# A two-layer transformer kernel on one core: who evicts the second attention's keys, queries and values

## The chip, the cores and the metric

The kernel runs on 1 core of one Trainium2 chip. The metric is the time of one execution on the device in microseconds (us), lower is better. Engines are named as in the profile: PE is TensorE (PEld its weight loads), DVE VectorE, ACT ScalarE, POOL GpSimd, SP SyncE.

## What is computed

2048 tokens of width 128 pass two layers. The first mixes in the frequency domain and has a gated feed-forward block; the second is plain attention over all 2048 tokens with 16 heads of width 8, then a mixture of 8 experts. Only the beginning of the second attention matters here:

```python
h = layernorm(x) * (1 + ca) + sa                 # 2048 x 128
qkv = einsum('bnd,ed->bne', h, qkv_w) + qkv_b
q, k, v = split(qkv.reshape(b, n, 16, 3 * 8), 3) # per head
attn = softmax(einsum('bhqd,bhkd->bhqk', q, k) * 8 ** -0.5)
out = einsum('bhqk,bhkd->bhqd', attn, v)
```

## The kernel before, in words

One program per engine, written out by hand; semaphores order the engines. Numbers of lines are those of the profile.

**The products.** Keys and queries are made as 32 "stacks": a stack is one f32 product of 128x512 (L787), for one of four head groups `hg` and one block `tb` of 512 tokens. In each head's 32 rows stand three copies of its 8 numbers, which carry a two-part (high and low) form: ScalarE copies the product with a mask as scale into `hi`, rounded to fp32r (L506), and VectorE computes product + bias - `hi` into `Ks` or `Qs` (L1257). The list `stacks` gives their order. The values are 16 tiles of 128x256, two to a PSUM bank (L796, `value_tiles`); VectorE adds the bias row `vb1` on the way into `V` (L1263). Stacks and values rotate through the PSUM banks 4 to 7.

**The first maxima.** The softmax needs the maximum of each query's scores before its main loop. `nat(k, pair)` on TensorE makes two 128x512 score products of 32 rows each (L811) in one of two pairs of banks; `maxima(k, pair)` on VectorE reduces them with one instruction over 1024 columns (L1269). Key positions k run from 0; 21 of them (`LEAD`), so 42 of these pairs, come before the main loop. I call the place of one pair a slot: slot 2k + pair. After k = 15 VectorE reduces the row maxima once more (`maximum(0)`), GpSimd splits them (`split_max(0)`), TensorE transposes them (`max_rows(0)`), ScalarE copies them to `mT`, and two DMAs from SP's queue put them into rows of `Qb`.

**The order.** Five stacks come first (`early`), then ScalarE copies the first queries into `Qb` and the slots begin. The function `between(slot)` says which of the other 27 stacks and the 8 pairs of value tiles stand behind which of the first 32 slots; TensorE and VectorE both follow it. Slots 32 to 41 have no such work; there `keep_busy` puts products without use between the pairs (46 of 128x512, L851, two of them directly ahead of the loop). The loop (`step(s)`, 256 steps) takes scores, exponentials on ScalarE into `probs`, products with `V`, and goes on with the maxima of later key positions.

Of the kernel before, what the change touches and what calls it, by code (L numbers as in the profile page):

```python
# [12 lines left out]
F32 = mybir.dt.float32  # L13
F32R = mybir.dt.float32r
BF16 = mybir.dt.bfloat16
ALU = mybir.AluOpType
# [3 lines left out]
P = 128  # L20
# [15 lines left out]
VW = 16  # L36
# [27 lines left out]
x2_ready kq_ready kq_hi kq_done v_ready v_copied q_filled busy_done bank_ready bank_read rows_read m_top m_step  # L64
# [5 lines left out]
def adaln_pair(nc, x_in, consts_in, mods_in, spectral_in, ffn_in, attn_in, moe_in, out):  # L70
    with ExitStack() as ctx:
        def sb(name, shape, dt=F32, where=ctx):
            return where.enter_context(nc.sbuf_tensor(name, shape, dt))
# [79 lines left out]
        with l1:  # L153
            Ks = sb("Ks", [P, HG, TOK], F32R, where=l1)
            Qs = sb("Qs", [P, HG, TOK], F32R, where=l1)
            Qb = sb("Qb", [P, HG, 512], F32R, where=l1)
            V = sb("V", [P, NT, H1 * VW], where=l1)
            hi = sb("hi", [P, 2, 512], F32R, where=l1)
            probs = sb("probs", [P, 16, 512], where=l1)
            mx = sb("mx", [P, 2, 4, 4, G4], where=l1)  # L160
            mn = sb("mn", [P, 16], where=l1)
            m2 = sb("m2", [P, 4, 8], where=l1)
            mhi = sb("mhi", [P, 16], F32R, where=l1)
            mT = sb("mT", [8, 512], F32R, where=l1)
            U = sb("U", [P, 512], where=l1)
            rden = sb("rden", [P, 4, G4], where=l1)

        l2 = ExitStack()
        with l2:
# [15 lines left out]
            gtT = sb("gtT", [8, 512], where=l2)  # L185
            acc = sb("acc", [P, 4, P], where=l2)


        def columns(tensor, pack):
            at, views = 0, {}  # L190
# [23 lines left out]
        def due(count):  # L214

            return not isinstance(count, int) or count > 0
# [43 lines left out]
        def wait_turn(engine, *what):  # L260
# [9 lines left out]
            + [(1, hg, 0) for hg in range(1, HG)] + [(0, hg, tb) for hg in range(2, HG) for tb in range(TB)] \  # L270
            + [(1, hg, tb) for hg in range(HG) for tb in range(1, TB)]
        early = 5

        def between(slot):
# [3 lines left out]
            n = len(stacks)  # L278
            return range(min(lo, n), min(hi_, n)), range(max(lo, n) - n, max(hi_, n) - n)


        groups = [(ri, j) for ri in range(2) for j in range(KV)]
# [31 lines left out]
        def _(pool):  # L314
# [32 lines left out]
            for hg in range(1, HG):  # L347
                pool.wait_ge(sem.kq_done, stacks.index((1, hg, 0)) + 1)
                fill(0, hg)
            split_max(0)  # L350
            pool.wait_ge(sem.kq_done, len(stacks))
            for grp in range(1, 16):
                split_max(grp)
# [5 lines left out]
        def _(act):  # L359
# [139 lines left out]
            ln_out(2)  # L499

            act.wait_ge(sem.attn_in, 16)
            for n, (kq, hg, tb) in enumerate(stacks):
                act.wait_ge(sem.kq_ready, n + 1)
                if due(n - 1):
                    act.wait_ge(sem.kq_done, n - 1)
                act.activation(hi[:, n % 2, :], bank(4 + n % 4), ACT.Identity, bias=(kb_lo, qb_lo)[kq][:, hg:hg + 1],  # L506
                               scale=cw[("lo_k", "lo_q")[kq]]).then_inc(sem.kq_hi, 1)
                if n == early - 1:

                    act.wait_ge(sem.kq_done, early)  # L510
                    act.activation(Qb[:, 0, :], Qs[:, 0, 0:512].bitcast(F32), ACT.Copy).then_inc(sem.first_filled, 1)


            def copy_max_rows(grp):

# [21 lines left out]
            copy_max_rows(0)  # L537
            for s in range(256):
                exps(s)
            act.wait_ge(sem.pv_ready, 256)  # L540
# [60 lines left out]
        def _(pe):  # L601
# [180 lines left out]

            def stack(n):
                kq, hg, tb = stacks[n]
                if due(n - 3):
                    pe.wait_ge(sem.kq_done, n - 3)
                pe.matmul(bank(4 + n % 4), aw[("kw1", "qw1")[kq]][:, hg * P:hg * P + P],  # L787
                          hT[:, tb * 512:tb * 512 + 512], start=True, stop=True).then_inc(sem.kq_ready, 1)

            def value_tiles(u):  # L790
                pe.wait_ge(sem.kq_done, min(len(stacks), len(stacks) - 3 + u))
                if due(u - 3):
                    pe.wait_ge(sem.v_copied, u - 3)
                for i in range(2):
                    t = 2 * u + i
                    last = pe.matmul(ps[:, 4 + u % 4, 256 * i:256 * i + 256], hT[:, t * P:t * P + P], aw["vw1"],  # L796
                                     start=True, stop=True)
                last.then_inc(sem.v_ready, 1)

            def nat(k, pair):  # L800
# [95 lines left out]
            for n in range(early):  # L896
                stack(n)
            pe.wait_ge(sem.kq_done, early)
            for k in range(16):
                for half in range(2):  # L900
                    nat(k, half)
                    some_stacks, some_values = between(2 * k + half)
                    for n in some_stacks:
                        stack(n)
                    for u in some_values:
                        value_tiles(u)
            pe.wait_ge(sem.v_copied, NT // 2 - 2)
            keep_busy(8)
            pe.wait_ge(sem.v_copied, NT // 2)
            for k in range(16, LEAD):  # L910
                for pair in range(2):
                    nat(k, pair)
# [112 lines left out]
        def _(dve):  # L1025
# [225 lines left out]
            ln_stats(2, TB - 1)  # L1251
            ln(2)

            def stack(n):
                kq, hg, tb = stacks[n]
                dve.wait_ge(sem.kq_hi, n + 1)
                dve.scalar_tensor_tensor(out=(Ks, Qs)[kq][:, hg, tb * 512:tb * 512 + 512], in0=bank(4 + n % 4),  # L1257
                                         scalar=(kb_one, aw["qb1"])[kq][:, hg:hg + 1], in1=hi[:, n % 2, :].bitcast(F32),
                                         op0=ALU.add, op1=ALU.subtract).then_inc(sem.kq_done, 1)

            def value_tiles(u):
                dve.wait_ge(sem.v_ready, u + 1)
                dve.tensor_tensor(V[:, 2 * u:2 * u + 2, :], bank(4 + u % 4).rearrange("p (t n) -> p t n", t=2),  # L1263
                                  wide(aw["vb1"], [P, 2, H1 * VW], 1), ALU.add).then_inc(sem.v_copied, 1)

            def maxima(k, pair):
                at = turn_bank("nat", k, pair)
                dve.wait_ge(sem.bank_ready, turn_at["nat", k, pair] + 1)
# [32 lines left out]
                if kt == turn_kt and s > 16:  # L1301
                    normalise(grp)

            for n in range(early):
                stack(n)
            for k in range(16):
                for half in range(2):
                    maxima(k, half)
                    some_stacks, some_values = between(2 * k + half)
                    for n in some_stacks:  # L1310
                        stack(n)
                    for u in some_values:
                        value_tiles(u)
            maximum(0)
            for pair in range(2):
                maxima(16, pair)

            dve.wait_ge(sem.v_copied, NT // 2)
            dve.memset(bank(6), 0.0).then_inc(sem.u_zero, 1)
            for k in range(17, LEAD):  # L1320
                for pair in range(2):
                    maxima(k, pair)
            for s in range(256):
                step(s)
            normalise(16)
# [182 lines left out]
```

## Time and profile before

| | us |
|---|---|
| median of three runs | 1224.33 |
| lowest and highest | 1223.57, 1225.33 |
| the profiled execution | 1223.92 |
| its span, first to last instruction | 1222.1 |
| VectorE busy | 829.3 (68%) |
| ScalarE busy | 813.3 (67%) |
| GpSimd busy | 28.9 (2%) |
| TensorE busy | 1129.2 (92%) |
| mean granted TensorE clock | 0.974 |

Times of instructions below are microseconds from the span's start. The difference of the profiled time and its span, 1.8 us, lies outside the first and last instruction.

### The profile page before, as it was taken

To read this page: it belongs to the slowest core of one execution; us is meant where nothing else is said; L and a number is where in the kernel's file an instruction comes from. 1 tells how busy PE (TensorE), PEld (TensorE's weight loads), DVE (VectorE), ACT (ScalarE), POOL (GpSimd) and SP (SyncE) were. 2 spreads that over 40 slices of the span, in tenths; PEclk is the share of its full clock that TensorE was granted. 3 is DMA by queue.
4 is the path that set the end of the run, shared out by engine and by line. 5 is a ranking of instruction groups with operands and counts; after the bars stand their busy time and mean duration, and the time that the engine had idled before them with its cause. 6 is when DMAs were issued, how large, how long until landed. Compare 5 with 4: busy or idle time off the path is not lost.

```text
span 1222.1 us, 21866 instructions
## 1 busy us (share of the span) xinstructions
PE 1129.2 (92%) x9020; PEld 634.8 (52%) x9020; DVE 829.3 (68%) x1172; ACT 813.3 (67%) x1495; POOL 28.9 (2%) x73
## 2 busy tenths in 40 slices
PE   4865999888999999999999999999999699999998
PEld 3534788732533333333333333333333379798887
DVE  3857333369999999999999999999930622222222
ACT  2646443344089999989999999999898554444342
POOL 0002000000000000000000000000000000000000
PEclk9996999979989999999999999999999899999999
DMA  9000000000000000000000000000000000000000
GB/s 383 21 1 0 1 1 1 1 0 1 1 2 2 2 2 2 1 2 2 2 2 2 2 2 2 2 2 2 2 2 2 1 1 1 10 1 9 6 3 9
DMA packets 5432, 14.84 MB, mean 12 GB/s; under 512 B 352, under 2 KB 4576, under 8 KB 4832
## 3 DMA queue, kind: packets, MB, share of 16 engines
q1 hardware_dynamic: 5056, 10.84, 2.3%
q10 hardware_dynamic: 288, 2.76, 0.5%
q8 instruction: 64, 1.05, 0.3%
q14 instruction: 24, 0.20, 0.1%
HBM read 12.29 MB, written 1.05 MB: 11 GB/s over the span
## 4 chain that ended last, share of the span: by engine, by line
DVE 48%; PE 46%; ACT 4%; issue 1%; DMA 1%; SPq 0%; DVEq 0%; ACTq 0%
DVE mx L1269 41%; PE ps L990 9%; PE ps L721 6%; PE ps L722 6%; PE ps L723 6%; PE ps L870 4%; PE ps L842 4%; PE ps L758 1%; PE ps L811 1%; PE ps L971 1%; PE ps L787 1%; DMA x<-x_in 1%; PE ps L851 1%; DVE Qs L1257 1%; DVE z L1042 1%
## 5 line engine op out<-in xcount | busy, mean ns | idle before, releaser
L1269 DVE TENSOR_REDUCE mx<-ps 128x2 f32<-128x1024 f32 x512 | 587.7, 1213 | 14.8 <-PE ps L811 14.1
L534 ACT ACTIVATE probs<-ps 128x512 f32<-128x512 f32 x1024 | 540.7, 598 | 57.3 <-PE ps L870 48.3
L870 PE MATMUL ps<-Qb,Ks 32*128 32x512 f32 x1024 | 328.7, 496 | 0.5 <-ACT probs L534 0.5
L842 PE MATMUL ps<-probs,V 128*16 128x256 f32 x4096 | 320.6, 386 | 7.1 <-ACT U L528 7.1
L811 PE MATMUL ps<-Ks,Qb 32*128 32x512 f32 x1024 | 257.3, 499 | 8.2 <-DVE mx L1269 5.2
L870 PEld LDWEIGHTS ps<-Qb,Ks 32*128 32x128 f32 x1024 | 150.5, 182 | 214.7 <-issue 124.7
L581 ACT ACTIVATE eh<-ps,MW 128x512 f32<-128x512 f32 x128 | 87.5, 688 | 83.4 <-PE ps L723 82.9
L842 PEld LDWEIGHTS ps<-probs,V 128*16 128x16 f32 x4096 | 67.2, 94 | 134.1 <-issue 76.5
L990 PEld LDWEIGHTS ps<-MW,eh 128*128 128x128 f32 x1024 | 118.3, 192 | 2.4
L811 PEld LDWEIGHTS ps<-Ks,Qb 32*128 32x128 f32 x1024 | 95.3, 182 | 46.1 <-DVE mx L1269 32.0
L990 PE MATMUL ps<-MW,eh 128*128 128x128 f32 x1024 | 119.2, 275 | 0.0
L1388 DVE SCALAR_TENSOR_TENSOR acc<-ps,gate,acc 128x128 f32<-128x128 f32 x128 | 36.0, 344 | 121.5 <-PE ps L990 121.1
L721 PE MATMUL ps<-hT,ew 128*128 (+1 forms) x128 | 53.1, 415 | 0.0
L1224 DVE TENSOR_TENSOR act_b<-bf,act_b 128x512 fp32r<-128x512 f32 x16 | 11.1, 692 | 58.9 <-ACT bf L478 58.9
L722 PE MATMUL ps<-hT,ew 128*128 (+1 forms) x128 | 50.1, 391 | 0.0
L723 PE MATMUL ps<-hT,ew 128*128 (+1 forms) x128 | 50.0, 390 | 0.0
L787 PE MATMUL ps<-hT,AW 128*128 128x512 f32 x64 | 38.5, 703 | 0.9 <-ACT hT L375 0.9
L1286 DVE RECIPROCAL rden<-ps 128x16 f32<-128x16 f32 x16 | 4.1, 257 | 49.3 <-PE ps L828 48.9
L484 ACT ACTIVATE act_c<-ps,FW 128x512 f32<-128x512 f32 x16 | 11.0, 686 | 27.5 <-PE ps L723 27.5
L721 PEld LDWEIGHTS ps<-hT,ew 128*128 128x128 f32 x128 | 24.1, 188 | 7.7 <-issue 3.4
L574 ACT ACTIVATE rh<-ps,MW 128x512 f32<-128x512 f32 x16 | 10.9, 688 | 24.8 <-PE ps L723 24.8
L711 PE MATMUL ps<-CW,z 128*128 128x128 f32 x48 | 12.5, 432 | 15.9 <-DVE z L1042 15.9
(218 smaller groups left out, 1085.9 us busy)
## 6 DMA issues: line engine op xcount, KB each, us to landing
MW<-moe_in SPq DMA_DIRECT2D x1, 4454.0 KB, 23.9
FW<-ffn_in SPq DMA_DIRECT2D x1, 2824.5 KB, 12.5
SW<-spectral_in ACTq DMA_DIRECT2D x1, 1479.5 KB, 9.9
DW<-mods_in ACTq DMA_DIRECT2D x1, 1219.0 KB, 6.4
x<-x_in SPq DMA_DIRECT2D x4, 256.0 KB, 10.9
out<-x SPq DMA_DIRECT2D x4, 256.0 KB, 2.3
AW<-attn_in SPq DMA_DIRECT2D x1, 836.5 KB, 13.8
Qb<-mT SPq DMA_DIRECT2D x32, 8.0 KB
```

The source lines that it names most:

```text
L534: act.activation(probs[:, 4 * (s % 4) + g, :], score(n), ACT.Exp, scale=SCALE1) \
L581: act.activation(eh[:, e % 2, fb, :], up_bank(fb), ACT.Relu, bias=mw["eb1"][:, col:col + 1]).then_inc(sem.eh_copied, 1)
L721: pe.matmul(to, w[0], v[0], start=start, stop=False)
L722: pe.matmul(to, w[0], v[1], start=False, stop=False)
L723: return pe.matmul(to, w[1], v[0], start=False, stop=stop)
L787: pe.matmul(bank(4 + n % 4), aw[("kw1", "qw1")[kq]][:, hg * P:hg * P + P], hT[:, tb * 512:tb * 512 + 512], start=True, stop=True).then_inc ...
L811: last = pe.matmul(bank(turn_bank("nat", k, pair) + g % 2), Qb[rows, hg, qt * P:qt * P + P], Ks[rows, hg, c * 512:c * 512 + 512], start=Tr ...
L842: last = pe.matmul(ps[32 * g:32 * g + VW, 6, queries], V[:, kt, col:col + VW], probs[:, 4 * (s % 4) + g, queries], start=(kt == 0 and half ...
L870: pe.matmul(score(n), Ks[rows, hg, kt * P:kt * P + P], Qb[rows, hg, :], start=True, stop=True).then_inc(sem.st_ready, 1)
L990: last = pe.matmul(ps[:, 2 + e % 2, qt * P:qt * P + P], eh[:, e % 2, fb, qt * P:qt * P + P], mw["ew2"][:, col:col + P], start=(fb == 0), s ...
L1269: dve.tensor_reduce(mx[:, k // 16 % 2, k % 16 // 4, k % 4, 2 * pair:2 * pair + 2], ps[:, at:at + 2, :], AX, ALU.max).then_inc(sem.bank_rea ...
L1388: dve.scalar_tensor_tensor(out=acc[:, qt, :], in0=ps[:, 2 + e % 2, qt * P:qt * P + P], scalar=gate[:, qt, e:e + 1], in1=acc[:, qt, :], op0 ...
```

## The change

VectorE does nothing for stacks and values any more. For a stack ScalarE makes both copies of the product, `hi` (masked, fp32r, L532 in the changed kernel) and `full` (with the whole bias, f32, L534); GpSimd subtracts one from the other into `Ks` or `Qs` (L362) and also does the three copies into `Qb` in the same program order. `full` and `hi` are four buffers each, laid in the first eight of the 16 slots of `probs`, which the exponentials use only later; for that ScalarE waits for all 32 subtractions ahead of its first exponential. The bias of the values is a one-row product (a row of ones times `vb1`, L832) that accumulates on each value tile, and ScalarE copies two tiles to `V`. The values stand after 20 stacks, not after all 32. The 35 late items are spread over 42 slots, not 32, and 44 of the 46 products of `keep_busy` are gone. A bank is free for TensorE when ScalarE has read it (`kq_full`, `v_copied`).

```diff
+        items = [("stack", n) for n in range(20)] + [("value", u) for u in range(NT // 2)] \
+            + [("stack", n) for n in range(20, len(stacks))]
         def between(slot):
-            total = len(stacks) - early + NT // 2
-            lo, hi_ = early + total * slot // 32, early + total * (slot + 1) // 32
...
+            total = len(items) - early
+            return items[early + total * slot // (2 * LEAD):early + total * (slot + 1) // (2 * LEAD)]
# GpSimd
+            def stack(n):
+                kq, hg, tb = stacks[n]
+                pool.wait_ge(sem.kq_hi, n + 1)
+                pool.wait_ge(sem.kq_full, n + 1)
+                pool.tensor_tensor((Ks, Qs)[kq][:, hg, tb * 512:tb * 512 + 512], full[:, n % 4, :], hi[:, n % 4, :].bitcast(F32),
+                                   ALU.subtract).then_inc(sem.kq_done, 1)
+                if kq and hg and tb == 0:
+                    pool.wait_ge(sem.kq_done, n + 1)
+                    fill(0, hg)
+            for n in range(early):
+                stack(n)
+            for slot in range(2 * LEAD):
+                for kind, n in between(slot):
+                    if kind == "stack":
+                        stack(n)
+                if slot == 33:
+                    split_max(0)
# ScalarE
+                if n > 3:
+                    act.wait_ge(sem.kq_done, n - 3)
+                act.activation(hi[:, n % 4, :], bank(item_bank("stack", n)), ACT.Identity, bias=(kb_lo, qb_lo)[kq][:, hg:hg + 1],
                                scale=cw[("lo_k", "lo_q")[kq]]).then_inc(sem.kq_hi, 1)
+                act.activation(full[:, n % 4, :], bank(item_bank("stack", n)), ACT.Identity,
+                               bias=(kb_one, aw["qb1"])[kq][:, hg:hg + 1]).then_inc(sem.kq_full, 1)
+            def value_tiles(u):
+                act.wait_ge(sem.v_ready, u + 1)
+                act.activation(V[:, 2 * u:2 * u + 2, :], bank(item_bank("value", u)).rearrange("p (t n) -> p t n", t=2),
+                               ACT.Copy).then_inc(sem.v_copied, 1)
# TensorE
+                    pe.matmul(to, hT[:, t * P:t * P + P], aw["vw1"], start=True, stop=False)
+                    last = pe.matmul(to, cw["ones"][0:1, :], aw["vb1"][0:1, :], start=False, stop=True)
...
-            pe.wait_ge(sem.v_copied, NT // 2 - 2)
-            keep_busy(8)
...
-                    if k > 16:
-                        keep_busy(3)
                 if k == 16:
-                    keep_busy(8)
                     max_rows(0)
-                    keep_busy(4)
+            pe.wait_ge(sem.kq_full, len(stacks))
             keep_busy(2).then_inc(sem.busy_done, 1)
# VectorE: stack and value_tiles are gone
+            for k in range(LEAD):
+                for pair in range(2):
+                    maxima(k, pair)
+                if k == 15:
+                    maximum(0)
+            dve.wait_ge(sem.kq_full, len(stacks))
             dve.wait_ge(sem.v_copied, NT // 2)
             dve.memset(bank(6), 0.0).then_inc(sem.u_zero, 1)
```

How the order moves on TensorE at the value tiles. In rows of an order, `ps<-hT,AW` is a stack, `ps<-Ks,Qb` a half of a score pair, `ps<-AW,hT` a value tile. Before:

```order
L811 MATMUL ps<-Ks,Qb 128x512 [waits bank_read]
L811 MATMUL ps<-Ks,Qb 128x512
L796 MATMUL ps<-AW,hT 128x256 [waits kq_done]
L796 MATMUL ps<-AW,hT 128x256
L811 MATMUL ps<-Ks,Qb 128x512 [waits bank_read]
```

After (`ps<-AW,CW` is the one-row product):

```order
L846 MATMUL ps<-Ks,Qb 128x512 [waits bank_read]
L846 MATMUL ps<-Ks,Qb 128x512
L831 MATMUL ps<-AW,hT 128x256 [waits kq_full]
L832 MATMUL ps<-AW,CW 128x256
L831 MATMUL ps<-AW,hT 128x256
L832 MATMUL ps<-AW,CW 128x256
L846 MATMUL ps<-Ks,Qb 128x512 [waits bank_read]
```

Each value tile has got a second product, and a pair of tiles is now four products between two score pairs.

On GpSimd, at slot 33, where the first row maxima are split. Before:

```order
L332 COPY Qb<-Qs 128x512 [waits kq_done] x3
L341 TENSOR_SCALAR mhi<-mn 128x16 [waits m_top]
L342 TENSOR_SCALAR m<-mn 128x4x4
L344 TENSOR_TENSOR m<-m,mhi 128x4x4 [waits m_step]
```

After:

```order
L362 TENSOR_TENSOR Ks<-probs 128x512 [waits kq_full,kq_hi] x8
L362 TENSOR_TENSOR Qs<-probs 128x512 [waits kq_full,kq_hi] x5
L352 TENSOR_SCALAR mhi<-mn 128x16 [waits m_top]
L353 TENSOR_SCALAR m<-mn 128x4x4
L355 TENSOR_TENSOR m<-m,mhi 128x4x4 [waits m_step]
L362 TENSOR_TENSOR Qs<-probs 128x512 [waits kq_full,kq_hi] x7
```

The split of the maxima, for which TensorE waits in `max_rows(0)`, now stands behind the 25th subtraction, that of the stack that TensorE issues directly ahead of that wait.

## Rows read from the trace of the kernel before

**Rows 1.** Groups of instructions by shape: busy us, mean ns, idle before and releaser.

```profile
L1269 DVE TENSOR_REDUCE mx<-ps 128x2 f32<-128x1024 f32 x512 | 587.7, 1213 | 14.8 <-PE ps L811 14.1
...
L581 ACT ACTIVATE eh<-ps,MW 128x512 f32<-128x512 f32 x128 | 87.5, 688 | 83.4 <-PE ps L723 82.9
...
L332 POOL CAST Qb<-Qs 128x512 fp32r<-128x512 f32 x15 | 9.2, 610 | 280.7 <-DVE Qs L1257 176.7 <-PE ps L870 103.9
```

**Rows 2.** Timeline of VectorE, stage of the stacks: start, us, instruction.

```profile
299.67 1.21 DVE L1269 TENSOR_REDUCE mx<-ps 128x2 f32<-128x1024 f32 x1
300.81 0.74 DVE L1257 SCALAR_TENSOR_TENSOR Qs<-ps,AW,hi 128x512 fp32r<-128x512 f32 x1
301.46 1.21 DVE L1269 TENSOR_REDUCE mx<-ps 128x2 f32<-128x1024 f32 x1
```

**Rows 3.** Timeline of TensorE, the same stage to the loop's first score, idle in brackets.

```profile
259.75 0.50 PE L811 MATMUL ps<-Ks,Qb 32*128 32x512 f32 x2 [2.41 <-ACT Qb L511]
...
263.82 0.79 PE L811 MATMUL ps<-Ks,Qb 32*128 32x512 f32 x2
...
266.55 0.79 PE L811 MATMUL ps<-Ks,Qb 32*128 32x512 f32 x2
...
299.58 1.98 PE L787 MATMUL ps<-hT,AW 128*128 128x512 f32 x4
301.50 0.50 PE L811 MATMUL ps<-Ks,Qb 32*128 32x512 f32 x2
301.92 1.13 PE L787 MATMUL ps<-hT,AW 128*128 128x512 f32 x2
302.98 0.50 PE L811 MATMUL ps<-Ks,Qb 32*128 32x512 f32 x2
...
317.89 1.99 PE L796 MATMUL ps<-AW,hT 128*128 128x256 f32 x8
319.79 2.11 PE L851 MATMUL ps<-Ks 128*128 128x512 f32 x8
...
324.53 0.60 PE L820 MATMUL ps<-CW,m 128*8 128x128 f32 x4
...
337.21 0.51 PE L870 MATMUL ps<-Qb,Ks 32*128 32x512 f32 x3
```

**Rows 4.** Timeline of ScalarE: two stretches of this stage, and one of a later norm.

```profile
253.19 0.78 ACT L506 ACTIVATE hi<-ps,kb_lo,CW 128x512 fp32r<-128x512 f32 x1 [2.23 <-PE ps L787]
...
258.98 0.63 ACT L511 ACTIVATE Qb<-Qs 128x512 fp32r<-128x512 f32 x1 [0.82 <-DVE Qs L1257]
...
300.75 1.67 ACT L506 ACTIVATE hi<-ps,qb_lo,CW 128x512 fp32r<-128x512 f32 x2 [1.01 <-PE ps L787]
...
969.34 0.77 ACT L380 ACTIVATE hT<-ps,modv,cv 128x512 fp32r<-128x512 f32 x1
970.00 0.78 ACT L375 ACTIVATE hT<-ps,modv,cv 128x512 f32<-128x512 f32 x1
```

**Rows 5.** Timeline of GpSimd: the weight split of the first layer; the split of maxima.

```profile
91.45 1.89 POOL L323 CAST h<-FW 128x2048 fp32r<-128x2048 f32 x1 [83.43 <-DVE x L1174]
93.42 4.50 POOL L325 TENSOR_TENSOR h<-FW,h 128x2048 fp32r<-128x2048 f32 x1
...
322.32 0.26 POOL L341 TENSOR_SCALAR mhi<-mn 128x16 fp32r<-128x16 f32 x1 [45.81 <-DVE mn L1277]
...
322.88 0.22 POOL L344 TENSOR_TENSOR m<-m,mhi 128x16 f32<-128x16 f32 x1
```

**Rows 6.** Timeline of TensorE in the experts: eight 8-row products, then 128-row ones.

```profile
996.59 1.15 PE L1010 MATMUL ps<-MW,gtT 8*128 8x128 f32 x8
997.68 3.84 PE L990 MATMUL ps<-MW,eh 128*128 128x128 f32 x32
```

**Rows 7.** Stretches of 1 us: length, TensorE busy (instructions), granted clock, DMA.

```profile
261.00:262.00 1.00, 1.00 (x4) 0.71 0.00 0
...
268.00:269.00 1.00, 1.00 (x4) 0.87 0.00 0
```

More of the change, by code:

```diff
@@ L63 @@
 yT_ready yT_copied idft_ready x1_ready u_ready t_ready ug_ready a_ready h_ready b_ready w3_ready w3_scaled
-x2_ready kq_ready kq_hi kq_done v_ready v_copied q_filled busy_done bank_ready bank_read rows_read m_top m_step
+x2_ready kq_ready kq_hi kq_full kq_done v_ready v_copied q_filled busy_done bank_ready bank_read rows_read m_top m_step
 first_filled mrow_in st_ready exp_done pv_ready u_copied u_zero u_rcp oT_ready oT_copied fc_ready
@@ L157, in adaln_pair @@
             V = sb("V", [P, NT, H1 * VW], where=l1)
-            hi = sb("hi", [P, 2, 512], F32R, where=l1)
             probs = sb("probs", [P, 16, 512], where=l1)
@@ L186, in adaln_pair @@
             acc = sb("acc", [P, 4, P], where=l2)
+        full, hi = probs[:, 0:4, :], probs[:, 4:8, :].bitcast(F32R)
         def columns(tensor, pack):
@@ L272, in adaln_pair, with item_bank, wait_item_bank @@
         early = 5
+        items = [("stack", n) for n in range(20)] + [("value", u) for u in range(NT // 2)] \
+            + [("stack", n) for n in range(20, len(stacks))]
+        item_at = {item: i for i, item in enumerate(items)}
         def between(slot):
-            total = len(stacks) - early + NT // 2
-            lo, hi_ = early + total * slot // 32, early + total * (slot + 1) // 32
-            n = len(stacks)
-            return range(min(lo, n), min(hi_, n)), range(max(lo, n) - n, max(hi_, n) - n)
+            total = len(items) - early
+            return items[early + total * slot // (2 * LEAD):early + total * (slot + 1) // (2 * LEAD)]
+        def item_bank(*what):
+            return 4 + item_at[what] % 4
+        def wait_item_bank(engine, *what):
+            if item_at[what] >= 4:
+                kind, n = items[item_at[what] - 4]
+                engine.wait_ge(sem.kq_full if kind == "stack" else sem.v_copied, n + 1)
         groups = [(ri, j) for ri in range(2) for j in range(KV)]
@@ L345, in split_max @@
                                    ALU.subtract).then_inc(sem.m_step, 1)
[L347 to L350, printed above, removed]
+            def stack(n):
[15 more added lines that the diff above has]
+                    split_max(0)
             pool.wait_ge(sem.kq_done, len(stacks))
@@ L501, in _, with stack @@
             act.wait_ge(sem.attn_in, 16)
-            for n, (kq, hg, tb) in enumerate(stacks):
+            def stack(n):
+                kq, hg, tb = stacks[n]
                 act.wait_ge(sem.kq_ready, n + 1)
-                if due(n - 1):
-                    act.wait_ge(sem.kq_done, n - 1)
-                act.activation(hi[:, n % 2, :], bank(4 + n % 4), ACT.Identity, bias=(kb_lo, qb_lo)[kq][:, hg:hg + 1],
+                if n > 3:
+                    act.wait_ge(sem.kq_done, n - 3)
+                act.activation(hi[:, n % 4, :], bank(item_bank("stack", n)), ACT.Identity, bias=(kb_lo, qb_lo)[kq][:, hg:hg + 1],
                                scale=cw[("lo_k", "lo_q")[kq]]).then_inc(sem.kq_hi, 1)
-                if n == early - 1:
-                    act.wait_ge(sem.kq_done, early)
-                    act.activation(Qb[:, 0, :], Qs[:, 0, 0:512].bitcast(F32), ACT.Copy).then_inc(sem.first_filled, 1)
+                act.activation(full[:, n % 4, :], bank(item_bank("stack", n)), ACT.Identity,
[4 more added lines that the diff above has]
+                               ACT.Copy).then_inc(sem.v_copied, 1)
             def copy_max_rows(grp):
@@ L535, in exps @@
                        .then_inc(sem.exp_done, 1)
-            copy_max_rows(0)
+            for n in range(early):
+                stack(n)
+            act.wait_ge(sem.kq_done, early)
+            act.activation(Qb[:, 0, :], Qs[:, 0, 0:512].bitcast(F32), ACT.Copy).then_inc(sem.first_filled, 1)
+            for slot in range(2 * LEAD):
+                for kind, n in between(slot):
+                    (stack if kind == "stack" else value_tiles)(n)
+                if slot == 33:
+                    copy_max_rows(0)
+            act.wait_ge(sem.kq_done, len(stacks))
             for s in range(256):
@@ L784, in stack @@
                 kq, hg, tb = stacks[n]
-                if due(n - 3):
-                    pe.wait_ge(sem.kq_done, n - 3)
-                pe.matmul(bank(4 + n % 4), aw[("kw1", "qw1")[kq]][:, hg * P:hg * P + P],
+                wait_item_bank(pe, "stack", n)
+                pe.matmul(bank(item_bank("stack", n)), aw[("kw1", "qw1")[kq]][:, hg * P:hg * P + P],
                           hT[:, tb * 512:tb * 512 + 512], start=True, stop=True).then_inc(sem.kq_ready, 1)
             def value_tiles(u):
-                pe.wait_ge(sem.kq_done, min(len(stacks), len(stacks) - 3 + u))
-                if due(u - 3):
-                    pe.wait_ge(sem.v_copied, u - 3)
+                wait_item_bank(pe, "value", u)
                 for i in range(2):
                     t = 2 * u + i
-                    last = pe.matmul(ps[:, 4 + u % 4, 256 * i:256 * i + 256], hT[:, t * P:t * P + P], aw["vw1"],
-                                     start=True, stop=True)
+                    to = ps[:, item_bank("value", u), 256 * i:256 * i + 256]
+                    pe.matmul(to, hT[:, t * P:t * P + P], aw["vw1"], start=True, stop=False)
+                    last = pe.matmul(to, cw["ones"][0:1, :], aw["vb1"][0:1, :], start=False, stop=True)
                 last.then_inc(sem.v_ready, 1)
@@ L898, in _ @@
             pe.wait_ge(sem.kq_done, early)
-            for k in range(16):
+            for k in range(LEAD):
                 for half in range(2):
                     nat(k, half)
[L902 to L906, printed above, removed]
-            pe.wait_ge(sem.v_copied, NT // 2 - 2)
-            keep_busy(8)
[L909 to L912, printed above, removed]
-                    if k > 16:
-                        keep_busy(3)
+                    for kind, n in between(2 * k + half):
+                        (stack if kind == "stack" else value_tiles)(n)
                 if k == 16:
-                    keep_busy(8)
                     max_rows(0)
-                    keep_busy(4)
+            pe.wait_ge(sem.kq_full, len(stacks))
             keep_busy(2).then_inc(sem.busy_done, 1)
@@ L1252, in _ @@
             ln(2)
[L1254 to L1264, printed above, removed]
             def maxima(k, pair):
@@ L1302, in step @@
                     normalise(grp)
[L1304 to L1316, printed above, removed]
+            for k in range(LEAD):
+                for pair in range(2):
[3 more added lines that the diff above has]
+            dve.wait_ge(sem.kq_full, len(stacks))
             dve.wait_ge(sem.v_copied, NT // 2)
             dve.memset(bank(6), 0.0).then_inc(sem.u_zero, 1)
-            for k in range(17, LEAD):
-                for pair in range(2):
-                    maxima(k, pair)
             for s in range(256):
```

## The prediction

> **What bounds the kernel now.** I read the page first (VectorE reduces 512 score pairs, 1213 ns each [rows 1]; nothing else of VectorE is near that), then the timelines of the stage in which the keys, queries and values are made, engine by engine, then the granted clock in it. The change touches nothing outside that stage, and the main loop that follows takes the same steps at the same prices, so the question is only when its first score starts. Before, that is at 337.21 [rows 3]; each microsecond by which it moves moves the end.
>
> In the stage VectorE alternates: from one reduction to what follows it are 1.14 us, from a subtraction to the next reduction 0.65 [rows 2]. With 27 late subtractions and 8 value additions beside the reductions it is hardly ever idle there (14.8 us in the whole run [rows 1]): a slot with a stack takes 1.79 us. That is what the change takes away, 40 instructions of about 0.65, some 26 us. But what is late next stands in TensorE's timeline. The reader should look at the one stretch where TensorE was not held by VectorE: after two stacks in a row it had a pair of maxima free. The score pair starts at 301.50, the stack at 301.92, the next score pair at 302.98 with no idle before it [rows 3]. So **TensorE alone needs 1.48 us for a slot with a stack**: 0.42 for the pair and 1.06 for the stack. The two stacks in a row took 1.92 from 299.58 to 301.50, so the first of them cost 0.86, and the 0.20 more of the second is the change from 128-row products to the 32-row pair. VectorE's 26 us can therefore give back only 0.31 per stack, and TensorE gets more work.
>
> **The change part by part**, as a sum of TensorE's time from the first score pair to the loop. TensorE becomes the engine that sets the pace; I cost the others at nothing only where their cover is named.
>
> *The start of the slots.* ScalarE's first copy starts at 253.19 as before. An activation with scale and bias occupies ScalarE for 0.66 when the next follows directly (969.34 to 970.00, duration 0.78) [rows 4]; one with bias alone lasts 0.09 less (0.688) [rows 1], so I take 0.58. ScalarE needs 1.24 for a stack, and the fifth `full` ends at 259.9. GpSimd's subtraction of 512 columns isn't in the trace. Its nearest rows: 4.50 us for the same operation on 2048 columns and 0.22 on 16 [rows 5], and 0.61 for a copy of 512 columns [rows 1]. The line through the two subtractions gives 1.27 us; scaled as the copies are (1.89 for 2048 columns, 0.61 for 512) it would be 1.45; below the copy's 0.61 it can't be. I take 1.27, since it is the same operation. The chain of five then ends at 261.3. From the start of the copy into `Qb`, 258.98, to the first pair, 259.75, were 0.77 us, behind a subtraction that ended at 258.94 [rows 3, 4]: the first pair now starts at 262.1, **2.4 us later**.
>
> *The slots.* 27 slots with a stack at 1.49 (0.43 + 1.06) are 40.2. Seven slots are empty, 0.43 each: 3.0. Of the value pairs, eight instructions (two pairs of tiles, two per tile) took 1.90 [rows 3], so 0.95 per pair of tiles before; the one-row products stream as many columns and double it to 1.90. To the score pair 0.20 are added, and the pair itself is 0.43: 2.53. Then each one-row product puts TensorE into few-row mode and back. For that I have two prices: the 0.20 above, and in the experts eight 8-row products took 1.09 to the next where 128-row ones take 0.12 each, so 0.13 to leave [rows 6]. Between the scores stand three such switches more; at 0.13 to 0.20 that is 0.4 to 0.6, at least 0. I take 0.4: 2.93 per slot, eight are 23.4. The transposes of the maxima: 0.5 [rows 3]. Together 67.1. VectorE's cover: a pair of reductions is 1.14, under every slot that has an item. ScalarE's: 1.24 per stack, under 1.49. GpSimd's: 1.27 and some 0.07 to start, under 1.49, with four buffers for the three slots where a copy of 0.61 into `Qb` comes along.
>
> *The pause at slot 33.* Before, the split of the maxima stood alone, and the eight busy products behind pair 33 covered it. Now it stands on GpSimd behind the 25th subtraction, whose stack TensorE has only just issued. From a stack's start to ScalarE's start are 1.17 (299.58 to 300.75) [rows 3, 4]; the two copies end 1.36 later, GpSimd starts 0.07 later and subtracts for 1.27, and the split takes 0.78 (322.32 to 323.10) [rows 5], so TensorE goes on 4.7 after the stack's start and not 1.06: **a pause of 3.65 us**. Behind it on TensorE are all later pairs, and with them VectorE, which is idle then. ScalarE waits in its copy to `mT` for the same transposes; its next stack comes only after them. The two DMAs into `Qb` have the last eight slots until the loop, longer than the four key positions of before.
>
> *The clock.* Behind the pause of 2.41 us ahead of the first pair, the granted clock fell at 261.4 to the lower of its two levels (1.2 GHz) and rose at 268.3, by the shares of the two stretches [rows 7]; a slot with a stack took 2.73 then (263.82 to 266.55) [rows 3]. The pause there is now 4.8 us long, and I expect the same fall: 6.2 us at the lower level lose 6.2 x (1 - 1.49/2.73) = 2.8. The pause at slot 33 is longer than the one that let the clock fall before, and no busy products are left around it: a second fall as long as that one, 6.8 us, loses 3.1.
>
> *The tail.* Behind the last stack TensorE waits for ScalarE's last `full` (2.6 from the stack's start, of which 1.06 are counted), then runs two busy products, 0.7 (2.11 for eight, and the last one's end) [rows 3]: 2.2. The last subtraction ends at about the time of the loop's first score, and the exponential's table load runs beside it; both cost nothing beyond 0.1. The 44 busy products that go (8, 8, 4 and 24 of them) are 10 us of TensorE, but they filled waits of slots 32 to 41, and those ten slots now hold 8 of the items.
>
> *Sum.* 262.1 + 67.1 + 2.8 + 3.65 + 3.1 + 2.2 = 340.9, against 337.2: the loop starts 3.7 us later. On the profiled 1223.9 that is **1227.6 us**. The median of the runs is 0.4 higher than the profiled one, so against it the forecast is 3.3 us, 0.27% slower.
>
> **The subtraction's engine.** What the trace shows for GpSimd is 4.50 us for a 2048-column subtraction [rows 5]. The Trainium skill, "GPSIMD Engine Reference", section 3.1, puts an elementwise operation with two inputs at 2.6 cycles per element, since both inputs share one read port, and its section 4.1 advises VectorE for such work; 512 columns would by that be about 1.11 us, an estimate from the page. With it the sum would come to about 1227.2. The trace agrees with the page at 2048 columns and shows no 512. It speaks against the change only through the two pauses, where the subtraction stands in a chain.
>
> **The rivals.**
>
> *The clock holds at slot 33.* Pauses differ in how they lie to the chip's decision, and TensorE is busy without a gap before this one, as it wasn't before the first. Then 3.1 us go: **1224.5**, no change. Against it: 2.41 us of waiting cost the clock already [rows 3, 7].
>
> *TensorE is cheaper than read, and the change not slower but faster.* The place is the value slots: if a one-row product costs its columns alone, with no change of mode, a value slot is 2.53, and eight of them give 3.2 back. With the clock held too it is **1221.3**. It decides from the point where both the switch is under 0.1 us and the pause leaves the clock alone; against it stand the 0.13 and 0.20 read from the rows.
>
> *VectorE was all that held the stage.* Were slots as short as VectorE's 1.14, 42 of them would take 48 us and the loop would start some 20 us earlier: **about 1205**. The free stretch at 301.50 to 302.98 speaks against it.
>
> *GpSimd sets the pace.* From a subtraction of 1.42 us (1.49 less 0.07) the items wait for GpSimd. Contention with VectorE could do it, though the reductions read PSUM alone. At 2.0 us: 27 x 0.58 = 15.7, three copies 2.1, three chains 0.73 each, less the empty slots (3.0) and the two low-clock times (5.9) that it hides in: 11.1 more, **about 1239**. The estimate by the copies, 1.45, lies just at the threshold.
>
> *The change doesn't do what it says* can't quite be: the order on VectorE has no such instruction left. What may be is that nothing of the relief is felt, and that is the forecast.
>
> **How the numbers follow.** The forecast 0.42, the clock holds 0.27, cheaper TensorE 0.13, VectorE alone 0.08, GpSimd 0.10. A measurement of this kernel can tell 0.2%, 2.4 us, from no change, so the marks are 1221.9 and 1226.8. The forecast is just above the upper one; some 0.06 of its chance lies below. Faster 0.13 + 0.08 = 0.21; same 0.27 + 0.06 = 0.33; slower 0.36 + 0.10 = 0.46. The range takes in both ends of the clock and mode prices (down to 1221, and 1219 with a subtraction under 1 us) and upward a second pause with a longer fall and a subtraction of 1.45 to 1.6: 1219 to 1234.5, which leaves out VectorE alone and most of the GpSimd case. The likeliest case's own range is 1225 to 1230.
>
> **What would show it.** Right: TensorE busy nearly without idle in slots 1 to 31, slots with a stack 1.49 apart, VectorE with idle before most reductions, released by TensorE; first pair at 262; the pause of 3.6 at the transposes; clock at the lower level after both pauses; first score of the loop at about 340.9. Wrong: value slots at 2.5, subtractions far from 1.27, a clock that stays up, or idle of TensorE released by ScalarE or GpSimd inside the slots.

## The result: 1246.7 us, 1.8% slower

| | before | changed |
|---|---|---|
| median us (runs) | 1223.95 (4) | 1246.72 (4), 1244.47 to 1248.55 |
| ratio, 95% interval | 1 | 1.0183, 1.0164 to 1.0202 |
| profiled execution, us | 1223.9 | 1246.6 |
| mean granted TensorE clock | 0.974 | 0.950 |
| first score of the main loop | 337.2 | 357.4 |

The forecast was 1227.6, its range ended at 1234.5. The sign was right, the size was not: of the 22.7 us between the two profiled executions 20.2 stand ahead of the loop's first score, where 3.7 were forecast.

The page of the changed kernel, the granted clock in 40 slices, and its costliest group and GpSimd's (columns as in [rows 1]):

```profile
PEclk9997999967579999999999999999999899999999
...
L1280 DVE TENSOR_REDUCE mx<-ps 128x2 f32<-128x1024 f32 x512 | 586.8, 1214 | 69.7 <-PE ps L846 69.6
...
L362 POOL TENSOR_TENSOR Ks<-probs 128x512 fp32r<-128x512 f32 x16 | 20.2, 1268 | 167.6 <-ACT probs L534 167.5
```

VectorE reduces at the same price as before, but now sits idle 69.7 us ahead of its reductions, all for TensorE, where [rows 1] had 14.8. GpSimd's subtraction is 1.268 us. And the clock has a dip in slices 10 to 12 (7, 5, 7), where the page of the kernel before has 9, 9, 8. TensorE's timeline shows what it does to the stage; the lines answer to [rows 3]:

```profile
261.91 0.80 PE L846 MATMUL ps<-Ks,Qb 32*128 32x512 f32 x4 [4.74 <-ACT Qb L568]
...
278.60 0.50 PE L846 MATMUL ps<-Ks,Qb 32*128 32x512 f32 x2
279.03 1.12 PE L823 MATMUL ps<-hT,AW 128*128 128x512 f32 x2
280.09 0.50 PE L846 MATMUL ps<-Ks,Qb 32*128 32x512 f32 x2
...
291.59 0.70 PE L831 MATMUL ps<-AW,hT 128*128 128x256 f32 x2
292.22 0.69 PE L832 MATMUL ps<-AW,CW 1*128 1x256 f32 x2
...
294.33 0.70 PE L831 MATMUL ps<-AW,hT 128*128 128x256 f32 x2
...
302.98 1.22 PE L831 MATMUL ps<-AW,hT 128*128 128x256 f32 x2
304.13 1.22 PE L832 MATMUL ps<-AW,CW 1*128 1x256 f32 x2
...
307.57 1.22 PE L831 MATMUL ps<-AW,hT 128*128 128x256 f32 x2
...
327.25 2.08 PE L823 MATMUL ps<-hT,AW 128*128 128x512 f32 x2
...
342.12 0.60 PE L855 MATMUL ps<-CW,m 128*8 128x128 f32 x4 [3.60 <-POOL m L355]
...
353.92 1.12 PE L823 MATMUL ps<-hT,AW 128*128 128x512 f32 x2
356.49 0.88 PE L886 MATMUL ps<-Ks 128*128 128x512 f32 x2 [1.45 <-ACT probs L534]
357.43 0.80 PE L905 MATMUL ps<-Qb,Ks 32*128 32x512 f32 x3
```

A slot with a stack is 1.49 (278.60 to 280.09), as read before. The first value slot is 2.74 (291.59 to 294.33), later ones 4.6 to 5.0 (302.98 to 307.57 is one of the shorter); the values go from 291.59 to 327.25. The granted clock in stretches (columns as in [rows 7]):

```profile
261.00:262.00 1.00, 0.09 (x4) 0.67 0.00 0
274.00:275.00 1.00, 1.00 (x2) 0.51 0.00 0
295.00:296.00 1.00, 1.00 (x4) 0.73 0.00 0
...
296.00:336.00 40.00, 40.00 (x83) 0.50 0.00 0
```

TensorE is busy for all of the 40 us from 296 to 336, without a gap, and gets half the clock, its lower level, 1.2 GHz. It had been at the upper level and without a gap for the 14 us ahead of the first value (277.1 to 291.6). No pause explains this fall; what is new there are the one-row products.

### The profile page after: what moved, and what is told of

Its sections match the earlier page's. It is cut to its first block, busy times and chain, and to the rows that moved or that the text cites. A ratio compares the mean times of both kernels' runs of the same rounds, so it can differ in the third digit from the quotient of the medians.

```text
span 1244.8 us, 21902 instructions
## 1 busy us (share of the span) xinstructions
PE 1148.7 (92%) x9008; PEld 639.0 (51%) x9008; DVE 804.4 (65%) x1132; ACT 836.2 (67%) x1535; POOL 69.3 (6%) x105
## 4 chain that ended last, share of the span: by engine, by line
PE 50%; DVE 43%; ACT 4%; issue 1%; DMA 1%; POOL 1%; SPq 0%; DVEq 0%; POOLq 0%; ACTq 0%
DVE mx L1280 38%; PE ps L1013 9%; PE ps L758 6%; PE ps L759 5%; PE ps L760 5%; PE ps L905 3%; PE ps L877 3%; PE ps L823 3%; PE ps L846 2%; PE ps L831 1%; PE ps L832 1%; PE ps L795 1%; PE ps L994 1%; DMA x<-x_in 1%; DVE z L1065 1%
## 5 line engine op out<-in xcount | busy, mean ns | idle before, releaser
L1280 DVE TENSOR_REDUCE mx<-ps 128x2 f32<-128x1024 f32 x512 | 586.8, 1214 | 69.7 <-PE ps L846 69.6
L846 PE MATMUL ps<-Ks,Qb 32*128 32x512 f32 x1024 | 263.6, 510 | 5.5 <-ACT Qb L568 4.7
L846 PEld LDWEIGHTS ps<-Ks,Qb 32*128 32x128 f32 x1024 | 97.9, 187 | 42.9 <-DVE mx L1280 29.4
L823 PE MATMUL ps<-hT,AW 128*128 128x512 f32 x64 | 45.9, 818 | 0.9 <-ACT hT L400 0.9
L362 POOL TENSOR_TENSOR Ks<-probs 128x512 fp32r<-128x512 f32 x16 | 20.2, 1268 | 167.6 <-ACT probs L534 167.5
L352 POOL TENSOR_SCALAR mhi<-mn 128x16 fp32r<-128x16 f32 x16 | 4.1, 254 | 439.5 <-DVE mn L1288 409.0
## 6 DMA issues: line engine op xcount, KB each, us to landing
MW<-moe_in SPq DMA_DIRECT2D x1, 4454.0 KB, 23.4
AW<-attn_in SPq DMA_DIRECT2D x1, 836.5 KB, 13.7
```

Of the source, the lines that this page charges most:

```text
L823: pe.matmul(bank(item_bank("stack", n)), aw[("kw1", "qw1")[kq]][:, hg * P:hg * P + P], hT[:, tb * 512:tb * 512 + 512], start=True, stop=Tr ...
L846: last = pe.matmul(bank(turn_bank("nat", k, pair) + g % 2), Qb[rows, hg, qt * P:qt * P + P], Ks[rows, hg, c * 512:c * 512 + 512], start=Tr ...
L1280: dve.tensor_reduce(mx[:, k // 16 % 2, k % 16 // 4, k % 4, 2 * pair:2 * pair + 2], ps[:, at:at + 2, :], AX, ALU.max).then_inc(sem.bank_rea ...
```

## The experiments

Two theories at this point. **The one-row products take the clock down** (they are half of TensorE's instructions in the values; the profile has them as 1*128 where a value product is 128*128). Or **the added work itself** is the cost, or the changes of mode that they bring, and the clock only follows something else.

### The bias product with 128 rows

Both operands get more rows; row 0 of the weights holds the ones, the other 127 are zeros (a new constant, `row0`). Columns, count and result stay.

```diff
-                    last = pe.matmul(to, cw["ones"][0:1, :], aw["vb1"][0:1, :], start=False, stop=True)
+                    last = pe.matmul(to, cw["row0"][0:128, :], aw["vb1"][0:128, :], start=False, stop=True)
```

> The one-row products get 128 rows: ones in row 0 and zeros in the other 127 as weights, the same columns and count. Theory (clock): products of one row let the granted clock fall at 295.5 in the changed kernel and hold it down through the values, 41 us; with 128 rows it stays at the upper level from the first values on, a value slot takes 2.5 us where it took 4.6 to 5.0, and the time is about 1227 (1246.6 less 19 to 20). Rival (the work): the added products and their place behind the score pairs are the cost, whatever their rows; then the time stays within 3 us of 1246.6. Second rival (the switch alone): only the changes between few-row and 128-row products go, 3 x 0.2 us x 8 = 5 us, time 1242.

Measured: 1225.85 us, ratio to before 1.0019 (0.9993 to 1.0046): 21 us less than the changed kernel (20 by the two ratios), from 127 more rows whose weights are zeros. The profiled execution is a longer one, 1230.5. Its timeline and clock in the values:

```profile
292.41 0.50 PE L846 MATMUL ps<-Ks,Qb 32*128 32x512 f32 x2
292.85 0.70 PE L831 MATMUL ps<-AW,hT 128*128 128x256 f32 x2
293.38 0.59 PE L832 MATMUL ps<-AW,CW 128*128 128x256 f32 x2
...
294.77 0.50 PE L846 MATMUL ps<-Ks,Qb 32*128 32x512 f32 x2
```

```profile
290.00:309.00 19.00, 19.00 (x86) 1.00 0.00 1
```

The slot is 2.36, the clock at its upper level through all values. The added work as such isn't where the 21 us were. The loop's first score is at 341.7; the forecast's sum had 340.9.

### The bias product with 32 rows

> The one-row products get 32 rows, 31 of them zeros: the same form of change between few-row and 128-row products, but more rows. If the change of mode holds the clock down, it is down from 295 to 337 as in the changed kernel, 1246. If the single row does, the clock stays up or is down for less of it, 1228 to 1240, with some 0.2 us of drain at each change left in the value slots.

Measured in one execution: 1228.0. The few-row form is still there, and the first value slot is again 2.74 (292.49 to 295.23), but the clock holds:

```profile
292.49 0.70 PE L831 MATMUL ps<-AW,hT 128*128 128x256 f32 x2
293.12 0.69 PE L832 MATMUL ps<-AW,CW 32*128 32x256 f32 x2
...
295.23 0.70 PE L831 MATMUL ps<-AW,hT 128*128 128x256 f32 x2
...
297.74 0.70 PE L831 MATMUL ps<-AW,hT 128*128 128x256 f32 x2
```

```profile
292.00:321.00 29.00, 28.99 (x106) 1.00 0.00 1
```

So the change of mode has a price of its own, 2.74 - 2.36 = 0.38 in the first slot and 0.15 in the next (295.23 to 297.74). From the first value to the first stack behind the last are 21.2 us (292.49 to 313.71) against 18.8 with 128 rows: 2.4 us in all, where the sum had taken 0.4 a slot, 3.2. It isn't what lowers the clock. With 32 rows the clock stayed up, with one it didn't; no run lies between.

### One part of the change alone, in the kernel before

The values' bias by one-row products; VectorE copies where it added. Nothing else is changed.

> The kernel before with one part of the change alone: the values' bias by one-row products, VectorE copies instead of adding. Slots there are held by VectorE at 1.73 us. Theory (clock): the clock falls in the values (308 to 322) and the ten slots behind them run partly at the lower level; eight value slots of about 4.6 instead of 1.73, less what is at the upper level, 12 to 22 us slower than 1223.9. Rival (the fall needs the crowded TensorE of the changed kernel): clock stays up, slots of 2.5 to 2.9, 6 to 9 us slower.

Measured in one execution: 1249.0, some 24 us slower than the kernel before on the same chip (1225.3), and more than the theory's 12 to 22. The clock in the values, and behind them:

```profile
308.00:313.00 5.00, 4.81 (x18) 1.00 0.00 0
314.00:348.00 34.00, 34.00 (x71) 0.50 0.00 0
348.00:349.00 1.00, 1.00 (x5) 0.95 0.00 0
```

The kernel before had the upper level in all of this; its stretch of the values:

```profile
308.00:320.00 12.00, 10.86 (x44) 1.00 0.00 0
```

The clock falls 5 us behind the first value at 308.6 and comes back 6 us into the busy products that follow the last value at 342. This one part costs about as much as the whole change. Not all of it is the clock: by the 32-row run eight such slots take 20.9 us at the upper level and took 8 x 1.73 = 13.8 here before, so some 7 us of the 24 are the products' own time, an estimate from these rows.

### The bias back on VectorE

TensorE has no bias product left, and ScalarE no copy of values.

```diff
+            def value_tiles(u):
+                dve.wait_ge(sem.v_ready, u + 1)
+                dve.tensor_tensor(V[:, 2 * u:2 * u + 2, :], bank(item_bank("value", u)).rearrange("p (t n) -> p t n", t=2),
+                                  wide(aw["vb1"], [P, 2, H1 * VW], 1), ALU.add).then_inc(sem.v_copied, 1)
```

> The values' bias goes back to VectorE (one addition per two tiles from PSUM, in the slots of the changed kernel), no one-row products. Theory (clock): the clock stays up as with 128 rows, and eight value slots are 0.95 us shorter than there: 1227 less 7.6, about 1219. The additions, 0.6 us each, lie in VectorE's idle time. Rival (the added products' time at any clock): 8 x 1.9 = 15 us at the lower level less, 1231.

Measured: 1230.2, 1.0033 (1.0014 to 1.0053), not 1219: the expectation failed. TensorE's work is 7 us less than with 128-row bias products, and the loop starts no earlier, at 341.4. TensorE now waits in the values, and the clock goes:

```profile
297.81 0.50 PE L846 MATMUL ps<-Ks,Qb 32*128 32x512 f32 x2 [0.17 <-DVE mx L1285]
299.54 0.79 PE L846 MATMUL ps<-Ks,Qb 32*128 32x512 f32 x2 [1.23 <-DVE mx L1285]
```

```profile
299.00:300.00 1.00, 0.46 (x2) 0.70 0.00 0
309.00:310.00 1.00, 1.00 (x2) 0.68 0.00 0
```

The 1.23 us of idle in the empty slot came right ahead of 10 us at the lower level. The additions, 0.6 us each, held VectorE, and the empty slot passed the wait on. That this wait is why the clock fell is argued from the order of the two, not tested. The time of the second theory, 1231, is met by accident: its reason, work at the lower level, would have had the clock low for all the values.

### The first pause filled

The next four start from the 128-row bias, to see what is left of the forecast's other terms. Here 18 products without use go into the wait ahead of the first score pair.

```diff
+            pe.wait_ge(sem.kq_done, 1)
+            for i in range(18):
+                pe.matmul(bank(i % 4), Ks[:, 0, 0:P], Ks[:, 0, 0:512], start=True, stop=True)
             pe.wait_ge(sem.kq_done, early)
```

> The changed kernel with the bias by 128-row products, and 18 products without use (128x512, fp32r) in TensorE's wait ahead of the first score pair (257.9 to 262.2 there). The clock theory: that idle time of 4.6 us costs what follows it, 262 to 272 at the lower level with four stack slots of 2.73 instead of 1.49; filled, it stays up, and the loop starts 4 to 5 us earlier than 341.7, time 1221 to 1222. Rival (the fall comes from the score pairs and copies themselves, or from the half-speed stage before): the clock falls at 262 all the same, time 1226.

Measured: 1223.4, 0.9978 (0.9965 to 0.9992). The clock holds from 262 on:

```profile
258.08 4.66 PE L935 MATMUL ps<-Ks 128*128 128x512 f32 x18
263.39 0.50 PE L846 MATMUL ps<-Ks,Qb 32*128 32x512 f32 x4 [0.65 <-ACT Qb L568]
```

```profile
262.00:290.00 28.00, 27.09 (x85) 1.00 0.00 1
```

In the profiled execution the loop starts at 332.5 instead of 341.7. That is more than the term (4 to 5 us), since the second fall was also short there, 317.4 to 320.9. The medians of the two versions differ by 2.4; the ratios, each to the kernel before on its own chip, by 0.41%, 5 us, since four of the ten executions of the 128-row bias were long ones. How long a fall behind the pause at slot 33 lasts varies: 3.4 us in the changed kernel (343.3 to 346.7), 3.4 here, 6.8 with 32 rows, 17 with the 128-row bias alone (320.0 to 337.1). The time of the 128-row bias varies from 1224.1 to 1236.2, and its longer executions have the lower mean clock (0.966 and 0.958 at these two), which fits.

### The split of the maxima earlier

The split goes ahead of one subtraction more, and the transposes and ScalarE's copy to `mT` go from slot 33 to slot 35.

```diff
-                if slot == 33:
+                if slot == 32:
                     split_max(0)
...
-                if k == 16:
+                if k == 17:
                     max_rows(0)
```

> The changed kernel with the bias by 128-row products; GpSimd splits the maxima behind the subtraction of slot 32 and not 33, and TensorE transposes them behind slot 35 and not 33. The pause of 3.6 us (316.8 to 320.4) should be under 0.7 us, and the lower clock from 319.9 to 337 should not come: 3 us of pause and 4 to 7 us of clock less, time 1216 to 1219. If the pause went but the clock fell there nevertheless, 1223.

Measured: 1223.6, 0.9980 (0.9961 to 1.0000), 2.3 less than the 128-row bias alone and not the 1216 to 1219 hoped for; it is the expectation's other case, 1223. The pause of 3.6 is gone, but another stands ahead of the second pair behind the transposes, and the clock still falls:

```profile
321.58 0.60 PE L855 MATMUL ps<-CW,m 128*8 128x128 f32 x4
322.11 0.51 PE L846 MATMUL ps<-Ks,Qb 32*128 32x512 f32 x2
323.74 0.50 PE L846 MATMUL ps<-Ks,Qb 32*128 32x512 f32 x2 [1.13 <-ACT mT L547]
```

```profile
326.00:335.00 9.00, 9.00 (x13) 0.50 0.00 0
```

The transposed maxima take a turn in the rotating banks, and ScalarE reads them out behind the copies of a stack. I had not looked at who frees that bank.

### The table load earlier

`full` and `hi` move to slots 8 to 15 of `probs`, and the wait for the 32nd subtraction stands ahead of the ninth exponential.

```diff
-        full, hi = probs[:, 0:4, :], probs[:, 4:8, :].bitcast(F32R)
+        full, hi = probs[:, 8:12, :], probs[:, 12:16, :].bitcast(F32R)
...
-            act.wait_ge(sem.kq_done, len(stacks))
             for s in range(256):
+                if s == 2:
+                    act.wait_ge(sem.kq_done, len(stacks))
                 exps(s)
```

> The changed kernel with the bias by 128-row products; the two copies use slots 8 to 15 of the probabilities and the wait for the last subtraction stands ahead of the ninth exponential, so that the exponentials' table is loaded before the loop's first score. The first exponential comes 0.5 us behind the first score as in the kernel before and not 2.2: 1.6 us less, 1224. If something else held the first exponential (the last subtraction), no change, 1226.

GpSimd's last subtraction in the changed kernel (first score 357.43):

```profile
356.58 1.28 POOL L362 TENSOR_TENSOR Qs<-probs 128x512 fp32r<-128x512 f32 x1 [0.23 <-ACT probs L534]
```

ScalarE's timeline there:

```profile
355.76 0.68 ACT L534 ACTIVATE probs<-ps,AW 128x512 f32<-128x512 f32 x1
358.30 1.28 ACT L562 ACT_TABLE_LOAD   x1 [1.86 <-PE ps L905]
359.60 5.02 ACT L562 ACTIVATE probs<-ps 128x512 f32<-128x512 f32 x10
```

and in this one (first score 336.62):

```profile
335.10 0.68 ACT L534 ACTIVATE probs<-ps,AW 128x512 f32<-128x512 f32 x1
335.80 1.28 ACT L562 ACT_TABLE_LOAD   x1
337.15 4.03 ACT L562 ACTIVATE probs<-ps 128x512 f32<-128x512 f32 x8
```

The load, which the forecast had put beside the last subtraction, had stood behind it (over at 357.86) and behind the first score as well, which is what the profile names as its releaser. With the wait moved it stands ahead of both. Here the first exponential comes 0.5 us behind the first score, not 2.2. The step is shown, which of the two waits had held the load is not; the time, 1225.4 with 1.0013 (0.9996 to 1.0030), can't tell 1.6 us from the scatter that the falls of the clock make.

### All pauses closed

The three edits together, and 7 products without use in the wait ahead of the loop.

```diff
+            at = turn_at["nat", LEAD - 1, 0]
+            pe.wait_ge(sem.bank_read, reads[at])
+            for i in range(7):
+                pe.matmul(bank(turn_bank("nat", LEAD - 1, 0) + i % 2), Ks[:, 0, 0:P], Ks[:, 0, 0:512], start=True, stop=True)
             pe.wait_ge(sem.kq_full, len(stacks))
```

> All together with 128-row bias products: first pause filled, split earlier, table load early, and 7 products without use in the wait ahead of the loop. TensorE's own work from the first pair at 262 is 27 x 1.49 + 8 x 2.36 + 7 x 0.33 + 0.5 = 62, and the tail 2.2: the loop starts near 326.5 if the clock stays up, 10.7 us earlier than in the kernel before, and the time is 1213 (before: 1224). If falls of the clock come elsewhere instead, 1216 to 1222.

Measured: 1214.5, 0.9913 (0.9897 to 0.9930), 0.9% faster than the kernel before, with less scatter (1213.7 to 1217.4). The loop starts at 328.8; 3.4 us of lower clock are left behind the wait of 1.13 for the maxima's copy, and 3.4 in the loop's first steps.

### The same with one-row products

> The version with all pauses closed, but with the one-row bias products of the changed kernel. If the one-row products bring the clock down by themselves, with TensorE busy without a gap for 28 us ahead of them, it falls within some microseconds of the first values at about 285 and stays low until stacks come again: some 18 to 20 us more than 1214.5, about 1233. If they only kept down what a pause had brought down, the clock stays up, the value slots cost 0.4 us more each, and the time is 1218.

Measured: 1235.1, 1.0078 (1.0053 to 1.0103), 20.6 us more than its 128-row twin (20.2 by the two ratios; they ran on different chips). Nothing but the rows of 16 products differs. TensorE ran at the upper level right up to the values, which begin at 287.57:

```profile
262.00:284.00 22.00, 21.21 (x65) 1.00 0.00 0
290.00:325.00 35.00, 35.00 (x75) 0.51 0.00 0
```

Its twin in the values, which begin at 286.20 there:

```profile
290.00:296.00 6.00, 6.00 (x27) 1.00 0.00 0
```

This closes the question of cause: TensorE's last wait ended at 265.3, the clock falls 25 us later with no pause ahead of it, and stays down with none. From the first score pair to the loop's first score are 84.6 us here and 66.7 in the twin: 17.9 of the difference. By the 32-row run 2.4 of them are the change of mode; the rest is the clock.

### All pauses closed, bias on VectorE

> The version with all pauses closed, but VectorE adds the values' bias and no bias product is left. TensorE's work is 8 x 0.87 = 7 us less, but VectorE then holds the value slots at 1.73 and TensorE waits there, in which the clock fell in the run with the bias on VectorE. If it falls again: 1213 to 1218. If it stays up: 1214.5 less (2.36 - 1.73) x 8 = 5, 1209.5.

Measured: 1211.2, 0.9888 (0.9851 to 0.9925), the lowest median, 1.1% under the kernel before; its interval overlaps that of the 128-row version with all pauses closed, so which of the two is faster isn't decided. The loop starts at 326.1. Between the two expectations: the clock does fall, three times (in the values, behind the transposes and in the loop), but for 3 us each.

## Why the prediction was wrong, point by point

**What bounds the stage: right.** TensorE sets the pace once VectorE is relieved; 1.49 per slot with a stack, idle of VectorE released by TensorE.

**The start of the slots: right.** 261.9 against 262.1; the subtraction is 1.267 to 1.268 against the 1.27 of the line through two rows. The Trainium skill, "GPSIMD Engine Reference", section 3.1, would have given about 1.11 by its 2.6 cycles per element, an estimate from the page; the measured number is 0.16 above it, and lies on the line through this case's 4.50 us for 2048 columns and 0.22 for 16.

**The value slots: the step that failed.** The sum had "each one-row product puts TensorE into few-row mode and back ... 2.93 per slot, eight are 23.4". At the upper level that was a little too much: the 32-row run, with the same changes of mode, has slots of 2.5 to 2.7, and its eight with one empty slot took 21.2 where the sum had 23.8. But it priced the one-row products as if they left the clock alone, and "the clock" had falls only behind pauses. The values took 35.7 us (291.59 to 327.25), with one empty slot, against 23.8: **11.9 more** (14.5 more than the 21.2). The clock then stayed down until 336.4, 9.1 us into the stacks behind them, where a slot is 2.73 and not 1.49: 9.1 x 0.454 = **4.1 more**. Together 16 of the 16.5 us by which the loop's start was missed.

**The first fall: right in kind, too short.** 13.1 us from the first pair at 261.9 to 275.0 instead of 6.2: 3.1 more. **The pause at slot 33: right**, 3.60 against 3.65. **The second fall:** 3.4 us instead of 6.8, 1.6 less, by luck: in other executions it was 6.8 and 17. The tail came to 3.5 from the last stack's start against 3.3, and the empty slots, 0.33 each and not 0.43, gave 0.7 back. 3.1 + 11.9 + 4.1 - 1.6 + 0.2 - 0.7, and 0.2 less at the first pair, make 16.8 (measured: 16.5).

**The table load "beside the last subtraction": wrong**, 1.6 us. At the loop's start the clock was low for 13.7 us (356.9 to 370.6) instead of 6.8 (339.9 to 346.8), but that cost nothing: from the first exponential to ScalarE's copy of `U` behind the last are 607.1 us (359.60 to 966.72) and were 607.2. The other 0.9 of the 2.5 us behind the first score came after the loop: from there to the copy to `scT` in the experts are 39.0 us and were 38.1, and the experts' first products ran at the lower level for 5.2 us (from 996.8), where they had for 3.2 (from 975.0).

**The rivals.** "The clock holds" and "cheaper TensorE" looked for surprises on the fast side of the same term. None asked whether the new products could lower the clock on a TensorE that is never idle. With that one thing taken out the sum came near, but in part by luck. The 128-row bias gave a loop's start at 341.7 for 340.9, and 1225.9 for 1227.6; in that execution the values took 5 us less than the sum had and the two falls cost 12 us (by the same 0.454) and not 5.9. The 32-row run, which keeps the changes of mode, gave 341.0 and 1228.0, once: values 2.6 less, falls 2.7 more.

The Trainium skill, "TensorE: Matmul & The Clock Gate", Part 1, says that the monitor sets the clock "based on how busy the PE has been recently", and its practical rule is about gaps. This trace agrees only if busy doesn't mean busy time: at a busy share of 1.00 for 40 us the granted clock was 0.50. What counted here was the number of rows of the products, one against 32 or 128; why it counts is not shown.

## What to carry to other kernels

A product with one row is cheap in columns and can be dear in clock: where a bias is accumulated by a product between other work, give it more rows, with weights of zero (32 were enough here), or leave it to an idle evicting engine. Read the granted clock over every stretch whose mix of products changes, not only behind pauses. And before moving work off an engine, price the slot of the next one alone: here VectorE's 26 us of relief were worth 0.3 us per slot on TensorE, and the new pauses took that back until they were closed (1225.9 with the 128-row bias, 1214.5 with the pauses closed too).

## What the runs showed of the hardware that I had not expected

- One-row f32 products (1x256, two per 128-row product pair) among other products: granted clock 0.50 at busy share 1.00, for 41 us in the changed kernel, 34 in the kernel before with this one part, 38 in the version with all pauses closed. It fell 2 to 5 us behind the first of them (292.2 to 295.5, 309.3 to 314.0, 288.2 to 290.5).
- With 32 rows, at the same time per product (0.69 for two), the clock stayed at 1.00 for the 29 us around the values, in one execution.
- A single wait of 1.13 to 1.23 us in a busy stretch stood ahead of falls of 3 to 10 us in four runs; in the one-row version with all pauses closed the same wait of 1.13 (over at 338.4) had none behind it for 13 us.
- The length of a fall behind one and the same pause differs between executions and versions, from 3 to 17 us; that this makes most of the scatter of their times fits their mean clocks but isn't shown.
